# Attention and feed-forward kernel: load order in the last stage, first unit's products moved two steps on, minus-one rows filled by GpSimd

## What is computed

```python
Q = _split_heads(x, H)
K = _split_heads(x @ Wk + bk, H)
V = _split_heads(x @ Wv + bv, H)
scores = jnp.einsum('bhqd,bhkd->bhqk', Q, K) + mask
attn = jax.nn.softmax(scores, axis=-1)
o = jnp.einsum('bhqk,bhkd->bhqd', attn, V)
y = _layernorm(x + (x + jax.nn.gelu(o, approximate=False) @ Wf + bf))
h = jax.nn.silu(y @ wg.T) * (y @ wu.T)
out = _layernorm(y + h @ wd.T)
```

## Time and profile before

| | |
|---|---|
| median of 3 runs | 2063.76 us (2058.99 to 2065.08) |
| time of the profiled execution | 2059.51 us |
| its span, first to last instruction | 2057.8 us |
| mean granted TensorE clock | 0.959 |
| PE busy | 1888.7 us (92%) |
| DVE busy | 1527.1 us (74%) |
| POOL busy | 1127.8 us (55%) |
| ACT busy | 1041.1 us (51%) |
| attention stage | about 52 to 1482 us |
| last stage | about 1482 to 2058 us |

### The profile page before, as it was taken

How to read it: one execution, slowest core, us unless ns; L and a number is a source line. 1 busy time by engine, 2 the same in 40 slices (tenths; PEclk the granted TensorE clock), 3 DMA queues, 4 the chain that set the end, 5 groups by cost and what they waited for, 6 DMA issues and landing times. The chain is left out here.

```text
span 2057.8 us, 38524 instructions
## 1 busy us (share of the span) xinstructions
PE 1888.7 (92%) x10304; PEld 975.6 (47%) x10304; DVE 1527.1 (74%) x3598; ACT 1041.1 (51%) x1523; POOL 1127.8 (55%) x1192
## 2 busy tenths in 40 slices
PE   6799999999999999999999999688879899999896
PEld 4344444444444444444444443233356666666664
DVE  3887878878788788887888878777156767676764
ACT  2255555555555555555555555444534545454543
POOL 0176776767767777677776776766511212121212
PEclk9799999999999999999999999987889999999998
DMA  9645536445364453654546544732147464747430
GB/s 306 200 135 154 174 111 193 150 142 184 105 190 156 139 180 113 183 152 146 173 123 178 153 144 131 199 93 59 53 114 188 120 188 118 191 118 192 119 105 21
DMA packets 260995, 303.24 MB, mean 147 GB/s; under 512 B 28065, under 2 KB 177697, under 8 KB 260913
## 3 DMA queue, kind: packets, MB, share of 16 engines
q1 hardware_dynamic: 260912, 302.25, 51.0%
HBM read 174.20 MB, written 127.93 MB: 147 GB/s over the span
## 5 line engine op out<-in xcount | busy, mean ns | idle before, releaser
L935 ACT ACTIVATE weights<-ring 128x1024 f32<-128x1024 f32 (+3 forms) x768 | 601.2, 810 | 370.1 <-PE ring L682 352.1
L652 POOL TENSOR_TENSOR weight_sum<-weight_sum,weights 128x512 f32<-128x512 f32 (+3 forms) x448 | 683.4, 1525 | 9.6
L682 PE MATMUL o_acc<-weights,v_pair 128*64 128x512 f32 (+3 forms) x3072 | 623.1, 513 | 6.5 <-POOL weights L630 5.9
L630 POOL TENSOR_SCALAR_AFFINE_SELECT weights<-weights 128x256 f32<-128x256 f32 x512 | 220.2, 435 | 356.5 <-ACT weights L935 350.2
L1085 DVE TENSOR_REDUCE part_max<-ring 128x2 f32<-128x1024 f32 x256 | 300.3, 1215 | 104.2 <-PE ring L682 104.2
L682 PE MATMUL ring<-q_stack,k_stack 50*128 50x512 f32 (+3 forms) x1536 | 315.6, 417 | 61.6 <-DVE rowmax L1093 27.6
L673 POOL TENSOR_TENSOR h_lo<-hidden,h_hi 128x512 f16<-128x512 f32 x96 | 114.1, 1190 | 449.8 <-ACT h_hi L903 449.8
L682 PE MATMUL ring<-k_stack,q_stack 48*128 48x512 f32 (+3 forms) x1536 | 307.7, 404 | 23.2 <-DMA k_stack<-k_rows 13.3
L1093 DVE CUSTOM_DVE_ANT_0 scrap<-ring,causal 128x128 bf16<-128x128 f32 (+3 forms) x512 | 229.3, 485 | 81.7 <-PE ring L682 81.3
L1093 DVE CUSTOM_DVE_ANT_0 scrap<-ring,causal,part_max 128x128 bf16<-128x128 f32 (+3 forms) x512 | 251.2, 547 | 47.7 <-PE ring L682 47.3
L682 PEld LDWEIGHTS o_acc<-weights,v_pair 128*64 128x64 f32 x3072 | 174.6, 138 | 228.6 <-issue 198.9
(11 more groups left out here) (105 smaller groups left out, 2162.6 us busy)
## 6 DMA issues: line engine op xcount, KB each, us to landing
v_pairs<-v_unit SPq DMA_DIRECT2D x64, 512.0 KB, 5.7
v_pair<-v_pairs SPq DMA_DIRECT2D x64, 512.0 KB, 5.5
o_heads<-o_pair SPq DMA_DIRECT2D x64, 512.0 KB, 5.2
g<-o_heads SPq DMA_DIRECT2D x16, 2048.0 KB, 8.2
den_wide<-reciprocals SPq DMA_DIRECT2D x32, 1024.0 KB, 16.7
q_stack<-q_rows SPq DMA_DIRECT2D x128, 192.0 KB, 3.6
k_stack<-k_rows SPq DMA_DIRECT2D x128, 192.0 KB, 4.2
q_rows<-x_hi SPq DMA_DIRECT2D x32, 512.0 KB, 5.1
```

The source lines that it names most:

```text
L630: pool.affine_select(out=diag, in_=diag, compare_op=ALU.is_ge, fill=0.0, base=0, pattern=[[0, 2], [1, P]], channel_multiplier=-1).then_inc ...
L652: pool.tensor_tensor(dst, other, W[t][:, :, :], ALU.add).then_inc(s_add, 1)
L682: return nc.tensor.matmul(o, l, r, start=start, stop=stop)
L935: nc.scalar.activation(W[t][:, :, :], bank_of("t", t)[:, :, 0:width_of(t)], ACT.Exp).then_inc(s_w, 1)
```

## The change

There are three edits.

1. In the last stage's `finish` on SyncE, the load of `den_wide` stands ahead of that of `g` and `xn`. Each keeps its own wait.
2. On VectorE the eight slices of `norm` of unit 0 are made in steps 64 and 65, four in burst 7 of each, in place of two in burst 6 of each of the steps 60 to 63.
3. The minus ones are written by eight memsets on GpSimd, each over 18 partitions of a `k_stack` half (16 rows of keys, which the first load overwrites later, and the two rows), each waiting for the one before. VectorE's memset of `minus_ones`, the tile, its semaphore and the eight DMAs go. SyncE waits for the memsets before the first load of the stacks; ScalarE's wait on them goes.

```diff
-            sp.wait_ge(s_minus, 1)
-            for i in range(RING):
-                for h in range(2):
-                    row = HSTEP * h + SROWS
-                    sp.dma_start(K[i][row:row + SHROWS, :].bitcast(F32), minus[:]).then_inc(s_krows, 16)
...
                 if a == 1:
 
+                    sp.wait_ge(s_krows, 2 * RING)
                     load_stacks(0, 0)
...
                 if r + 2 < UNITS:
+                    load_dn(r + 2, it)
+                if r + 2 < UNITS:
                     load_g(r + 2, it)
-                if r + 2 < UNITS:
-                    load_dn(r + 2, it)
...
+            pool.wait_ge(s_const, 4)
+            for i in range(RING):
+                for h in range(2):
+                    if i + h:
+                        pool.wait_ge(s_krows, 2 * i + h)
+                    low = HSTEP * h + SQ
+                    pool.memset(K[i][low:HSTEP * h + SROWS + SHROWS, :].bitcast(F32), -1.0).then_inc(s_krows, 1)
...
-            pe.wait_ge(s_krows, 16 * 2 * RING)
+            pe.wait_ge(s_krows, 2 * RING)
...
-            act.wait_ge(s_krows, 16 * 2 * RING)
...
-            v.memset(minus[:], -1.0).then_inc(s_minus, 1)
...
-                    if b == 6 and PAIRS - 4 <= r < PAIRS:
-                        norm(0, 0, range(2 * (r - PAIRS + 4), 2 * (r - PAIRS + 5)))
...
+                    if b == 7 and PAIRS <= r < PAIRS + 2:
+                        norm(0, 0, range(4 * (r - PAIRS), 4 * (r - PAIRS + 1)))
```

More of the change, by code:

```diff
@@ L174, in build @@
         wi_in = [sb(f"wi_in{i}", [P, DC * FH], I32, lctx) for i in range(3)]
-        minus = sb("minus_ones", [SHROWS, S], F32, lctx)
         lctx.close()
@@ L222, in build @@
         s_const = sem("constants_ready")
-        s_minus = sem("minus_ones_ready")
-        s_krows = sem("k_shift_rows_loaded")
+        s_krows = sem("k_shift_rows_set")
         s_w_hi = sem("weights_hi_ready")
```

## The result

| | before | after |
|---|---|---|
| median of 4 runs | 2061.38 us (2057.0 to 2065.08) | 2000.38 us (1997.72 to 2004.08) |
| ratio, with its 95% interval | | 0.9695 [0.9671, 0.9720] |
| time of the profiled execution | 2059.51 us | 2004.08 us |
| its span | 2057.8 us | 2002.3 us |
| mean granted TensorE clock | 0.959 | 0.971 |

The changed kernel is 3.0% faster, 61 us between the medians. The span is cut by the same landmarks in both traces: the starts of VectorE's sums (line 1127), one in each attention step, and the issue of the load of `g` for unit 2, the first of the loads of `g` that `finish` makes.

A forecast was written before the change was run, and what follows sets the result against it. TensorE, busy 92% of the span, was taken as the bound, with time to win only in its standstills and low clock. -50 - 15.6 - 0.7 = -66.3 us on 2059.51 gave 1993, median put at 1995 us, range 1985 to 2004.

The forecast's parts named there:

- Edit 1, -50: Last stage: loading den_wide earlier removes the wait and low clock, -50 us, between -30 and -53.
- Edit 2, -15.6: Attention stage's end: moving unit 0's products gives -15.1 - 4 + 3.5 = -15.6 us, between -22 and -1.
- The price on GpSimd: Steps 64 and 65: the moved products slow GpSimd's sums and masks, +3.5 us, bounds 0 and 13.8.
- another 4 us for the step without scores: Fourth of the steps freed of products: no more scores after it, so another -4 us, between 0 and -7.
- Rival (b): Steps 64 and 65: the products cost as much as they saved, GpSimd being on the path; 2010 us, chance 0.10.
- Edit 3, -0.7: Kernel start: fewer SyncE issues let the next xt be requested earlier, -0.7 us, between -2 and +2.
- The bound of +2: Kernel start: upper bound in case the eight memsets slow VectorE's splits in the first 14 us, +2 us.
- (a): Last stage: another wait, for g, xn or the silu_gate chain, replaces the removed one; 2016 or 2009 us, chance 0.14.
- (d): Last stage: g, queued behind den_wide, lands late and the kernel gets slower; 2090 us at 36 us landing, chance 0.02.
- the 0.15: Last stage: estimated loss of 0.15 us a unit, 2 us in all, for chains that come nearer.
- two chains: Last stage: hidden of f = 3 and the last h_lo tile before the down product, each with some tenths of room.
- (c): Last stage: total DMA traffic, not den_wide itself, causes the wait, so reordering gains nothing; 2045 us, chance 0.06.

The follow-up runs named there:

- e1_order: Kernel before with only the last stage's load of den_wide put ahead of g: 2012.51 us, ratio 0.9741.
- e2_products: Kernel before with only unit 0's eight norm products moved to steps 64 and 65: 2049.75 us, ratio 0.9916.
- e7_narrow: Changed kernel with unit 0's eight products in steps 64 and 65 cut to one column each: 1995.73 us, one run.
- e3_minus: Kernel before with only the minus ones written by eight GpSimd memsets: 2065.31 us, ratio 1.0009.
- e6_den_late: Changed kernel with den_wide still ahead of g but held until g's own waits have ended: 2062.67 us, ratio 0.9983.
- e10_one_later: Kernel before, old load order, each last-stage norm product put behind the next hidden tile: 2040.96 us, ratio 0.9888.
- e4_after: The repeat: the changed kernel run again without any edit: 2000.91 us, ratio 0.9698.
- e9_start: Changed kernel with step 58's bulk loads spread over four steps, unit 1's den_wide a step later, add_x of two tiles before unit 1's products: 1990.63 us.
- e5_memset_kept: Changed kernel with VectorE's memset of the unused minus_ones tile, the tile and its semaphore kept: 1997.64 us, one run.

## Why the prediction was right, point by point

The forecast of 1995 us was met at 2000.38, inside the forecast's own range of 1985 to 2004. Against its own starting value, the forecast was -68.8 us; between the medians of the result it is -61.0.

**Edit 1, -50.** The trace has -50.0 us from the load of `g` for unit 2 on, e1_order alone -52 us by its medians. Every link held: `den_wide` about 20 us ahead of `g` (1574.61 and 1594.62), no wait for it, units of 30.6 us against 30.45 + 0.15 in the working, clock 1.00. That the price of a unit was read from the windows (34.14 over 12 units), and not from TensorE's 2.7 us of waiting alone, is what made it right: by the waits' own 37.2 us a quarter would have been missed.

**Edit 2, -15.6.** The four steps were put at -19.1 and gave -14.4 in the first profile and -18.9 in the repeat; e2_products alone is -15 us by its medians and -17 by its ratio. The price on GpSimd was put at +3.5 and is 4.3 by e7_narrow, and +4.1 and +4.2 in the stretch behind step 64 of the two profiles. The row for a pair of products (0.86 us) gave four fifths of it: it was read in the place that the products left, where the instructions of GpSimd beside them were the same. GpSimd itself is slowed by 3.0 us, a little less than the forecast; what the working left out is that TensorE's granted clock is lower there too. The working was right to take another 4 us for the step without scores: 16.6 us, against 20.4 for the others. Rival (b), that the price eats up the gain, is refuted by the same numbers: from step 60 to the load of `g` 10.3 us were won in the first profile (14.4 - 4.1) and 14.7 in the repeat.

**Edit 3, -0.7.** The sign is not settled: 1.0009 [0.9994, 1.0025] is between -1 and +5 us. The first score product starts at 52.24 us for 52.61 in the first profile, but at 52.77 in e3_minus, so the gain at the start is not shown either. The loop lost 1.3 us, which no line of the working had, and which the trace before could not show. The step that failed is thus the one that ended the account of edit 3 with "VectorE's removed memset lay in idle time": its time was idle, its absence was not free. The bound of +2 was put there for another reason, slower splits of VectorE at the start. They are real, and hidden:

```profile
2.33 8.57 POOL L617 MEMSET k_stack<- 18x1024 f32 x8
...
4.62 1.21 DVE L1045 CAST x_hi<-xt 128x1024 fp32r<-128x1024 f32 x1 [3.62 <-DMA xt<-in_xT]
5.87 1.23 DVE L1049 TENSOR_TENSOR x_lo<-xt,x_hi 128x1024 fp32r<-128x1024 f32 x1
...
27.67 0.50 PE L684 MATMUL ring<-x_hi,wk_hi 128*128 128x512 f32 x1 [2.10 <-DVE x_lo L1049]
```

TensorE's second unit starts at 27.67 after a wait of 2.10, where the earlier trace rows has 28.27 and 3.76; its first unit had begun 1 us later, at 8.88 for 7.85. The earlier input and the slower splits nearly cancel.

**The rivals.** What (a) and (d) feared, `g` as the new last one, happened once in 14: in the first unit, where `den_wide` of unit 2 is issued only 6 us ahead of `g`, right behind the last store of reciprocals, and `den_wide` of unit 3 follows 3.3 us behind `g`, at 1504.39. `g` lands 19.4 us after its issue there.

```profile
1495.41 1.28 SPq L547 DMA_DIRECT2D den_wide<-reciprocals  x2
...
1501.08 0.40 SPq L534 DMA_DIRECT2D g<-o_heads  x1
```

```profile
1520.56 0.82 DVE L1148 TENSOR_TENSOR g<-g,den_wide 128x512 f32<-128x512 f32 x1 [2.48 <-DMA g<-o_heads]
...
1522.04 0.39 PE L684 MATMUL o_acc<-y_hi,wg_sb 128*128 128x512 f16 x1 [1.86 <-DVE hidden L1230]
```

It costs 1.9 us of TensorE. The working had subtracted 2 us, but for something else, 0.15 us in each unit. That term is there by itself: the later units take 30.6 us each, as forecast, while the first takes 32.2. That two losses were there, and the total still came out at -50.0, is in part luck. For the 0.15 the working had named two chains; the view of waits, which lists pieces from 0.15 us on, has none of TensorE in the later units up to the load for unit 15, so whether those chains cost it is not shown. e6_den_late shows `g` as the last one in every unit, at more than the price of edit 1. (c) is refuted by e6_den_late and e10_one_later together.

**The size, term by term.** The span was forecast to shrink by 66.3 us and shrank by 55.5 in the first profile and by 61.9 in the repeat. The 10.8 us between forecast and first profile are: 4.7 in steps 60 to 63 (the low clock), 0.6 behind step 64, 2.3 in steps 57 to 59, 1.5 in the loop, 1.8 up to step 2. In the repeat it is 4.4: 0.2, 0.7, 1.4, 2.1 and 0.6, and 0.6 back in the last stage. The loop's share and that behind step 64 stand in both: terms that were left out or sized too low. Much of the rest is TensorE's granted clock, step by step (length in us, clock):

| step | before | first profile after | e4_after |
|---|---|---|---|
| 56 | 22.1, 0.92 | 22.1, 0.92 | 23.2, 0.85 |
| 57 | 20.4, 1.00 | 20.4, 1.00 | 22.0, 0.92 |
| 58 | 20.5, 1.00 | 23.0, 0.85 | 20.4, 1.00 |
| 59 | 30.9, 0.78 | 30.7, 0.78 | 30.8, 0.78 |
| 60 | 23.6, 0.86 | 23.3, 0.85 | 20.5, 1.00 |
| 61 | 26.2, 0.74 | 22.0, 0.92 | 20.4, 1.00 |

Apart from step 59, and from 60 and 61 before the change, a step of this table takes 20.4 us at 1.00, 22.0 at 0.92 and some 23.2 at 0.85. So the 2.3 us of steps 57 to 59 are a fall of the clock in step 58, the 1.4 of the repeat one in step 57, and 1.1 of the repeat's 2.1 in the loop one in step 56. These are swings that the working, which took such steps at 20.42 us, had no term for. What makes the clock fall in one step or another is open. The stretch up to step 2 spreads as widely without edit 3 (98.2 in e1_order) as with it (96.7 and 97.9), so it is charged to no edit.

## What to carry to other kernels

Where one engine issues all loads in order, as here, it is the point at which a load's own wait ends that decides where it should stand: a load that is free early belongs ahead of one that is free late, and large loads issued in one go hold up all small ones behind them (10 us in step 59 here, in a place that no waiting row of the last stage pointed to). A stall on an in-order engine is charged to the instruction that waits, but is paid by what is queued behind it, so read the whole chain up to the engine that sets the time, and price it by the length of a unit and not by the wait. Read the granted clock of each stretch before you explain a difference of 1 to 5 us between two profiles. Work that is moved off the bounding engine's path costs what it does to the engine that is on the path at its new place; the row for that was there, in the old place.

## What the runs showed of the hardware

- **GpSimd's memsets slow some operations of VectorE and not others.** Beside the memsets the first cast of `x_hi` took 1.21 us; the kernel before has 0.69 for it (row below). The casts of `wk_hi` and `wv_hi` took 1.00 and 1.92 us for 0.42 and 1.23, the last with the memsets beside its first half only. The subtractions `x_lo` and `wk_lo`, which have two inputs in SBUF, took 1.23 and 0.69 us in both. The Trainium skill, page SBUF — State Buffer, section SBUF: two separate sides, has VectorE's fast modes share a port pair with any GpSimd operation, and two-input operations only with one that reads SBUF, which a memset does not: on which operations are slowed, the traces agree.

```profile
4.68 0.69 DVE L1045 CAST x_hi<-xt 128x1024 fp32r<-128x1024 f32 x1 [2.61 <-DMA xt<-in_xT]
```

- **The price of a VectorE product beside GpSimd** is 4.3 us for eight (e7_narrow), and each product itself takes 1.2 to 1.8 us (4.88 and 7.01 us for four) for 0.68 alone. The forecast's 3.5 came from a row. The same section of the Trainium skill, in which each would hold GpSimd for its whole instruction, gave 5.5. The trace does not bear out so full a hold, and the measurement decides: GpSimd's busy time grew by 3.0 us. The four products of step 64 (0.68 us each alone) and the two sums and two masks beside them (2.36 and 0.41 us each alone) would take 8.3 us one after the other, and were over in 7.3 (1441.73 to 1449.01).
- **TensorE's clock** fell behind two waits of 1.71 and 0.58 us in step 60 in one execution of a kernel, and not behind the same two waits in another of the same kernel. That explains 4.5 us between two profiles, the size of an effect that one would otherwise read as the change's. e2_products, with those products moved too, shows the same fall in steps 60 and 61, e9_start in steps 61 and 62.
- **An unused instruction ahead of a loop** was worth 0.1 us in every fourth step, 1.3 us in all (the changed kernel and e5_memset_kept, the latter one run).
